# The first combine weights go from SBUF to SBUF instead of through DRAM, and four steps of the handover to the experts change their order

## What is computed

```
x = x + tanh(g_xattn) * attention(layernorm(x), ctx)   # 16 heads of width 8, on itself and on ctx, gated per head
h = layernorm(x)
scores = sigmoid(h @ gate_w.T)                         # 64 experts in 8 groups
pick 4 groups by the sum of their two best biased scores, then 8 experts within them
w = scores of the picked / their sum * 2.5             # the combine weights, 0 for the others
y = sum over e of w[:, e] * ((silu(h @ Wg[e]) * (h @ Wu[e])) @ Wd[e])    # e: 64 experts of width 64
x = x + tanh(g_ffn) * (y + shared expert(h))
```

## Time and profile before

| | before |
|---|---|
| median of three runs | 873.26 us |
| profiled execution | 871.21 us |
| its span | 868.8 us |
| PE busy | 835.1 us (96%) |
| POOL busy | 636.8 us (73%) |
| DVE busy | 696.4 us (80%) |
| ACT busy | 567.8 us (65%) |

### The profile page before, as it was taken

How to read it: one execution, slowest core, us unless ns; L and a number is a source line. 1 busy time by engine, 2 the same in 40 slices (tenths; PEclk the granted TensorE clock), 3 DMA queues, 4 the chain that set the end, 5 groups by cost and what they waited for, 6 DMA issues and landing times.

```text
span 868.8 us, 20168 instructions
## 1 busy us (share of the span) xinstructions
PE 835.1 (96%) x6733; PEld 646.6 (74%) x6733; DVE 696.4 (80%) x1656; ACT 567.8 (65%) x964; POOL 636.8 (73%) x602
## 2 busy tenths in 40 slices
PE   5899999999999899999999999999999999999997
PEld 3476777776766677888888887877887888888885
DVE  6888899998888768787778887967987887886655
ACT  3378788887777756566566557557556656656554
POOL 2577888888873368887787787777788688788785
PEclk9999999999999999999999999999999999999999
DMA  5677677677653166556555654755655655556652
GB/s 132 182 182 185 179 200 186 181 200 179 161 168 92 30 149 148 131 136 148 136 129 131 146 132 120 170 130 122 156 125 132 149 142 119 145 135 146 136 137 61
DMA packets 113746, 125.26 MB, mean 144 GB/s; under 512 B 28000, under 2 KB 76064, under 8 KB 112208
## 3 DMA queue, kind: packets, MB, share of 16 engines
q1 hardware_dynamic: 110768, 123.47, 57.6%
q10 hardware_dynamic: 2880, 0.59, 0.4%
HBM read 103.55 MB, written 19.96 MB: 142 GB/s over the span
## 4 chain that ended last, share of the span: by engine, by line
PE 61%; DMA 5%; issue 4%; DVE 3%; POOL 3%; ACT 2%; SPq 1%; POOLq 0%; DVEq 0%; ACTq 0%
PE bank L1961 18%; PE bank L1962 17%; PE bank L1963 17%; DMA cwb<-wts_scratch 3%; PE bank L1305 2%; DMA stack_k<-k_scratch 1%; POOL hid L1640 1%; PE bank L1292 1%; PE bank L1279 1%; PE bank L1261 1%; DMA x_scratch<-x 1%; DVE mx L984 1%; ACT prob L787 1%; DVE hlo L1874 0%; PE bank L1938 0%
## 5 line engine op out<-in xcount | busy, mean ns | idle before, releaser
L1640 POOL TENSOR_TENSOR hid<-act,cwb 128x512 f32<-128x512 f32 x264 | 423.7, 1618 | 129.3 <-DVE act L1866 67.9
L1866 DVE TENSOR_TENSOR act<-silu,bank 128x512 f32<-128x512 f32 (+1 forms) x264 | 179.7, 681 | 109.4 <-ACT silu L1693 83.6
L1693 ACT ACTIVATE silu<-bank 128x512 f32<-128x512 f32 x256 | 152.5, 596 | 162.4 <-PE bank L1963 161.5
L1874 DVE TENSOR_TENSOR hlo<-hid,hhi 128x512 fp32r<-128x512 f32 x256 | 209.9, 820 | 14.2 <-ACT hhi L1699 14.0
L1961 PE MATMUL bank<-xhi,weights_hi 128*128 128x512 f32 x520 | 206.8, 398 | 0.7 <-ACT silu L1693 0.7
L1963 PE MATMUL bank<-xlo,weights_hi 128*128 128x512 f32 x520 | 204.2, 393 | 0.0
L1962 PE MATMUL bank<-xhi,weights_lo 128*128 128x512 f32 x520 | 204.0, 392 | 0.0
L1699 ACT ACTIVATE hhi<-hid 128x512 fp32r<-128x512 f32 (+1 forms) x264 | 165.4, 627 | 33.2 <-POOL hid L1640 29.2
L984 DVE TENSOR_REDUCE mx<-bank 128x4 f32<-128x512 f32 x256 | 167.3, 684 | 15.4 <-PE bank L1279 11.4
L787 ACT ACTIVATE prob<-bank 128x1024 f32<-128x1024 f32 x128 | 131.0, 1024 | 58.3 <-PE bank L1292 56.2
L1961 PEld LDWEIGHTS bank<-xhi,weights_hi 128*128 128x128 f32 x520 | 97.6, 188 | 22.8 <-ACT silu L1693 1.8
(11 more groups left out here) (235 smaller groups left out, 999.5 us busy)
## 6 DMA issues: line engine op xcount, KB each, us to landing
cwb<-wts_scratch SPq DMA_DIRECT2D x174, 384.0 KB, 5.4
stack_k<-k_scratch SPq DMA_DIRECT2D x30, 384.0 KB
k_scratch<-parts_k SPq DMA_DIRECT2D x15, 384.0 KB, 3.3
stack_q<-q_scratch SPq DMA_DIRECT2D x30, 192.0 KB
k_scratch<-parts_k SPq DMA_DIRECT2D x15, 256.0 KB, 3.9
q_scratch<-parts_q SPq DMA_DIRECT2D x15, 192.0 KB, 2.1
xin<-in_x_dram SPq DMA_DIRECT2D x16, 128.0 KB, 2.5
cin<-in_ctx_dram SPq DMA_DIRECT2D x16, 128.0 KB, 2.5
```

The costliest lines, as they stand in the source:

```text
L1640: pool.tensor_tensor(h_buf[k][:], a_buf[k][:], cwb[slot][:, q % GP, :], ALU.mult).then_inc(h_ok, 1)
L1693: act.activation(s_buf[k % RS][:], g_bank[k % 2][:], ACT.Silu).then_inc(s_ok, 1)
L1866: nc.vector.tensor_tensor(a_buf[k % RS][at], s_buf[k % RS][at], u_bank[k % 3][at], ALU.mult).then_inc(a_ok, 1)
L1874: nc.vector.tensor_tensor(hlo[k % RH][:], h_buf[k % RS][:], hhi[k % RH][:].bitcast(F32), ALU.subtract).then_inc(hl_ok, 1)
```

## The change

On PE, `first_turn_w` moves behind the last `weighted` units. On ACT, `copy_o` of the last entry moves from the expert body to the end of the attention stage, `first_wT` follows it, and the silu table is loaded behind both. On SP, the first group is spread by six DMAs, each of which reads one row of `f_wT` in SBUF and writes it to 64 partitions of `cwb[0]`; pair 0, pair 1 and pair 2 raise three semaphores (`cw_two` is new). The store to `wts_d` comes behind pair 0, and SP waits for it ahead of group 1, which still comes from DRAM. The wait for group 0 ahead of group 1 goes. `load_res(0)`, with its wait for all x2 stores, moves behind the load of group 4. POOL waits for each of the first three pairs by itself.

```
--- before
+++ after
@@ attention, on_sp, after the last body
-        sp.wait_ge(fwt_ev, 1)
-        sp.dma_start(wts_d[0], f_wT[:]).then_inc(fwt_st, 16)
-        sp.wait_ge(fwt_st, 16)
         sp.wait_ge(lo_ok, SPLITS * NC)
...
-        for gr, q0, q1, done in ((0, 0, 1, cw_one), (0, 1, GP, cw_in[0]), (1, 0, GP, cw_in[1])):
-            if gr == 1:
-                sp.wait_ge(cw_in[0], 32)
+        sp.wait_ge(fwt_ev, 1)
+        for q, done in ((0, cw_one), (1, cw_two), (2, cw_in[0])):
             for half in range(2):
-                sp.dma_start(cwb[gr][half * F:(half + 1) * F, q0:q1, :],
-                             wts_v[0][half][GP * gr + q0:GP * gr + q1].unsqueeze(0).to_broadcast([F, q1 - q0, T])
-                             ).then_inc(done, 16)
+                e = 2 * q + half
+                sp.dma_start(cwb[0][half * F:(half + 1) * F, q, :],
+                             f_wT[e:e + 1, :].unsqueeze(1).to_broadcast([1, F, T])).then_inc(done, 16)
+            if q == 0:
+                sp.dma_start(wts_d[0], f_wT[:]).then_inc(fwt_st, 16)
+        sp.wait_ge(fwt_st, 16)
+        for half in range(2):
+            sp.dma_start(cwb[1][half * F:(half + 1) * F, :, :],
+                         wts_v[0][half][GP:2 * GP].unsqueeze(0).to_broadcast([F, GP, T])).then_inc(cw_in[1], 16)
         store_x2(NC - 1, 1)
@@ attention, on_act: round 3 of the last entry, and after the last body
-                    if last and k == 3 and r == 3:
-                        first_wT()
...
+        copy_o(NB - 1, 1)
+        first_wT()
         act.wait_ge(warm_ok, 1)
         act.activation(warm[:], zero[:], ACT.Silu).then_inc(warm_ok, 1)
@@ attention, on_pe: round 3 of the last entry, and after the last body
-                    if last and k == 3 and r == 3:
-                        first_turn_w()
...
         for u in range(LAG):
             weighted(NB - 1, 1, u + UNITS - LAG, NC - 1, 1)
+        first_turn_w()
@@ experts, on_sp
-        for i in range(2):
-            sp.wait_ge(v["x2_st"][i], 16 * (NB // 4))
-        load_res(0)
-
...
                 for gr in range(2, GROUPS):
                     load_cwb(c, gr, (GROUPS * j + gr) % 2)
+                    if first and gr == F_GROUP - 1:
+                        for i in range(2):
+                            sp.wait_ge(v["x2_st"][i], 16 * (NB // 4))
+                        load_res(0)
@@ experts, on_pool, hidden
             if first and q == 0:
                 pool.wait_ge(cw_one, 32)
-            if q == (1 if first and q < GP else q // GP * GP):
+            if first and q == 1:
+                pool.wait_ge(cw_two, 32)
+            if q == (2 if first and q < GP else q // GP * GP):
                 wait(pool, cw_in[slot], 32 * (GROUPS * g + (GROUPS * j + q // GP) // 2 + 1))
@@ experts, on_act, body
-                    if first and q == 0:
-                        copy_o(NB - 1, 1)
```

More of the change, by code:

```diff
@@ L131, in build @@
         cw_in = [sem(f"cwb_loaded{i}") for i in range(2)]
-        cw_one = sem("first_pair_of_cwb_loaded")
+        cw_one, cw_two = sem("first_pair_of_cwb_loaded"), sem("second_pair_of_cwb_loaded")
         GP = 3
@@ L161, in _ @@
         def _(act):
-            v["experts_act"](act, *v["attention_act"](act))
+            v["experts_act"](act, v["attention_act"](act))
         @block.vector
@@ L179, in attention @@
     w_raw, w_lo, w_hi, w_in = v["w_raw"], v["w_lo"], v["w_hi"], v["w_in"]
-    cw_one = v["cw_one"]
+    cw_one, cw_two = v["cw_one"], v["cw_two"]
     NEX, NP, gwT, wts_d, cw_in, cwb, GP = (v[n] for n in ("NEX", "NP", "gwT", "wts_d", "cw_in", "cwb", "GP"))
@@ L908, in on_act @@
         body(LOOPS - 1, 0)
+        copy_o(NB - 1, 1)
+        first_wT()
         act.wait_ge(warm_ok, 1)
         act.activation(warm[:], zero[:], ACT.Silu).then_inc(warm_ok, 1)
-        return copy_o, copy_att
+        return copy_att
     def on_dve(dve):
@@ L1654, in on_pool, with on_act @@
         body(LOOPS - 1, True)
-    def on_act(act, copy_o, copy_att):
+    def on_act(act, copy_att):
         def norm(c):
```

## The result

The changed kernel takes 890.29 us (median of 4 runs, 887.39 to 892.49), the kernel before in the same comparison 873.37. The ratio is 1.0173 with a 95% interval of 1.014 to 1.0205. The profiled execution after took 892.49 us, its span is 889.9. Of the 21.1 us between the two spans, 3.8 were lost ahead of the handover, in instructions that the change doesn't touch: in the attention stage PE's waits for the stack transfers sum to 6.8 us there and to 3.0 before. The tail was 571.8 us and is 589.1, which is 17.3 us more.

A forecast was written before the change was run, and what follows sets the result against it. PE, 96% busy, bounds the kernel, so its idling at the handover to the experts reaches the end whole. V of 29.7 us minus 7.9 gives +21.8, 871.21 to 893.0 us; forecast's own range 888 to 898, full range 867 to 898.

The forecast's parts named there:

- V: Time of the six spreads from SBUF: 29.7 us at 26.5 GB/s for a pair, with ends of 4.0 and 59 us.
- the sum: hid(3) at 306.4 + V, so V − 7.9 in all with 0.7 off for the silu: +21.8 us.
- Four waits on PE, 25 us: PE would wait for hlo in four pieces between 300 and 340 us, some 25 us together.
- SP issues one in at most 0.6 us: On SP, all seven DMAs would be out by about 302.9 even at 0.6 us each.
- The copies: Moved copies and turn of weights remove two PE waits of 0.5 us; at most 1.0 us, all lent.
- f_wT 0.1 later: On ACT, f_wT stands behind the copy of o and is ready at about 298.85, 0.1 us later.
- the silu: PE's wait of 0.69 us for a late silu at 327.62 would go, taking 0.7 us off.
- later x2 load: Group 2 no longer held by the x2 store: hid(6) within some 5 us of hid(3), late silu gone.
- missing wait ahead of group 1: On SP, group 1 follows in the queue without waiting for group 0's landing, taking 4.0 us at 197 GB/s.
- As from DRAM: Rival: the spread runs at 197 GB/s, V 4.0 us, −3.9 us, at most 3.8 gained, 867.4 us; chance 0.25.
- Slow, but less: Rival: the spread runs at 34 to 75 GB/s, V 23 to 10.5 us, +15 to +2.6 us; chance 0.1.
- The waits cost more than themselves: Rival: long PE waits drop the clock to 1.2 GHz, leading to 897 us; slower still, chance 0.06.

The follow-up runs named there:

- e2: The kernel before with only the spread from SBUF added, behind the store and its wait; ratio 1.0223 to the kernel before.
- e1: The change with its six spreads reading the DRAM scratch instead of SBUF, all other edits kept; ratio 0.9936 to the kernel before.
- e3: The change with the six spreads reading rows of f_wT four apart (0, 4, 8, 12, 16, 20); ratio 1.0075 to the kernel before.
- e9: The change with the two rows of each pair 32 apart and pairs four apart; one run, 889.23 us (before 874.21).
- e5: The kernel before with only the change's moved copies and turn of the weights on PE and ACT; ratio 0.9985 to the kernel before.
- e6: The kernel before with only SP's two edits: no wait ahead of group 1, x2 load behind group 4; ratio 0.9961.
- e4: The change with each of the six transfers reading 64 partitions of f_wT once instead of one 64 times; ratio 0.9916 to the kernel before.
- e8: The change without the spread from SBUF, pair 0 spread by PE matmuls and an ACT copy, the rest from DRAM; ratio 0.997 to the kernel before.

## Why the prediction was right, and where its terms were off

*Place and direction: right.* The loss lies in the rate of the spread and nowhere else: e2 shows it with that edit alone, e1 shows it gone without it.

*V was some 4 us too long.* The forecast had 33.2 us from f_wT to hid(2) (30.7 of them for the six spreads and the store); hid(2) came after 29.7, which is 3.5 less. The last of pair 2 moved beside group 1, so hid(3) came 3.0 us behind hid(2), where the sum had 4.0. Together that is the 4.5 us between +21.8 and the +17.3 of the tail. The value of 26.5 GB/s for a pair was right (27 measured), the way to it was not, and that the two agree is luck. I had given each partition 13 GB/s because eight took 106 together, and those eight were written, not read. e3 shows that two rows four apart pass a pair in 5.2 to 5.4 us, about 262 KB / 5.3 us = 49 GB/s or 25 for one partition, and that neighbours share that amount. Pair 2 reads rows 4 and 5, which share with none of the rows 0 to 3, so it ran partly beside pair 1 (38 GB/s from 322 to 329 us) and took 7.7 us, not 10. The prediction's formula had all pairs in line.

The Trainium skill, page "SBUF — State Buffer", section "Door 1: The DMA port swizzle", was the better guide to the size: a port of about 27 GB/s for four neighbours and the four 32 partitions above. The measurements agree on all three counts (27 GB/s on rows 0 to 3, sharing at a distance of 32 in e9, none at a distance of four in e3). The burst of 16 KB that took 106 GB/s still doesn't fit the Trainium skill's table there, by which an estimate for its two ports is 54; no run here explains it.

*Four waits on PE, 25 us.* There were three, 15.7 us. hid(3) came 4.5 us sooner than in the sum, as above, and PE's busy time is 5.0 us longer: products at the lower clock fill part of what the sum had as waiting. When the down product of pair 3 could start, PE was only just through with them.

*SP issues one in at most 0.6 us: wrong, without a price.* The issues took up to 5.75 us (below). What stood behind them in SP's queue would probably have waited for the DMA engines in any case; no run tests it.

*The copies, f_wT 0.1 later, the turn of o, the silu: right.* f_wT was ready 1.8 us behind the start of `f_rep` in both profiles. The waits at the turn and for the copy of o are gone, and so is that for the silu. e5 shows the first two as lent. The later x2 load and the missing wait ahead of group 1 were worth 2.8 us of chunk 0 in e6, where 1.5 to 2.2 were expected; the sum named 0.7 for the silu and had the missing wait within hid(3).

*The rivals.* "As from DRAM" is what e4 did with a wide source: PE's waits fell to 0.4 us, but the tail lost 5.5 us (4.6 in chunk 0), more than the 3.8 that the prediction named as the most. "Slow, but less" is e3, +7.2, inside the +2.6 to +15 that the prediction gave for it. "The waits cost more than themselves": the clock did fall, and its price is some 0.4 us, because the slow products lie within waits for hlo.

## What to carry to other kernels

Here a transfer's rate was set by how many source partitions it reads and which: 64 copies of one SBUF row went at 27 GB/s, of one DRAM row at 197, and 64 SBUF rows at 194. A round trip through DRAM of 2 us is cheaper than a spread from a single SBUF partition as soon as more than some 65 KB are spread (an estimate: 2.07 us over the difference of 1/27 and 1/197); where the round trip itself is in the way, PE can spread a column while it turns it, at the cost of a copy. And an edit that removes a wait in front of a slower supplier is only lent: look for the next product of that supplier before counting it.

## What the runs showed of the hardware beside it

SP's issue of a DMA isn't of fixed length. The chain of waits after shows SP at the spreads (start us, us); the first spread's issue took 0.54 us, the later ones, with slow transfers ahead, up to 5.75 (the store among them, at 305.66, again 0.54). Before, from DRAM, none took longer than 0.62 in this place.

```profile
302.68 0.54 SPq L561
...
303.27 2.34 SPq L561
...
306.24 4.36 SPq L561
...
310.64 5.75 SPq L561
...
316.43 3.25 SPq L561
...
319.72 3.62 SPq L561
```

The granted clock went from 1.00 to 0.50, the lower level of 1.2 GHz, at 312 us, after PE had done nothing since 310.0. It was back at 1.00 from 323 to 325 us, after PE had worked from 317.6 to 321.8, and fell again while PE waited until 327.3. Before, no slice of the profile was below the top digit. In some profiles it was also low near the start, where nothing had been changed, as in that of e8 (its granted clock in 40 slices follows). What that costs isn't shown: the tail began 0.4 us (e5) to 6.2 us (e4) later than before in profiles with such a slice, and 3.8 (the change) and 4.1 us (e3) later in profiles without one.

```profile
PEclk9599999999999999999999999999999999999999
```
